# Attention with 16-feature heads: three banks for the scores by key and one for the output, in place of two and two

## The reference

```
# block 1 (stage Aatt): 4 batch entries, T = 1024, 16 heads of 16 features, rotary positions, causal
att = jnp.einsum('bhqd,bhkd->bhqk', q, k) / jnp.sqrt(jnp.float32(HS))
att = jnp.where(causal, att, jnp.float32(-1000000000.0))
att = jax.nn.softmax(att, axis=-1)
y = jnp.einsum('bhqk,bhkd->bhqd', att, v)
...
# block 3 (stage Catt): the same sizes, no mask, a bias by relative position
att = jnp.einsum('bhqd,bhkd->bhqk', q, k) * (1.0 / math.sqrt(HS))
att = att + compute_bias(rel_emb, t, t)
att = jax.nn.softmax(att, axis=-1)
o = jnp.einsum('bhqk,bhkd->bhqd', att, v)
```

## Time and profile before

| | us |
|---|---|
| median of 3 timed runs (lowest to highest) | 7709.58 (7699.38 to 7716.36) |
| profiled execution, its own time | 7715.76 |
| its span, first to last instruction | 7714.1 |
| Aatt, scores from the first to the last start | 287.8 to 956.6 |
| Catt, scores from the first to the last start | 3105.7 to 4032.4 |
| busy in the whole span: PE, DVE, ACT, POOL | 6384.6, 4755.7, 2770.5, 1252.2 |

### The profile page before, as it was taken

One profiled execution on the slowest core, in us unless ns is written; L12 is line 12 of the kernel. 1 busy time (PEld: TensorE's weight loads), 2 busy tenths in 40 slices (PEclk: granted clock), 3 DMA queues, 4 the chain that ended last, 5 costly groups with the idle time before them and its releaser, 6 DMA issues. The chain is left out here.

```text
span 7714.1 us, 120187 instructions
## 1 busy us (share of the span) xinstructions
PE 6384.6 (83%) x31364; PEld 3277.2 (42%) x31364; DVE 4755.7 (62%) x12029; ACT 2770.5 (36%) x6066; POOL 1252.2 (16%) x779
## 2 busy tenths in 40 slices
PE   6788858989987976899994387887996888998979
PEld 2333334655455533222222263334553455544555
DVE  4656557733763534899985747984335764347635
ACT  0255514712463210466661104541110354224611
POOL 1100016100620002000000003550002431015100
PEclk9899979989998988899997599998998999999999
DMA  5422245541455245333323211114222455324541
GB/s 176 115 64 65 54 132 155 181 141 59 147 169 185 75 176 199 103 81 76 87 55 108 90 70 53 37 39 132 66 63 83 132 163 175 93 88 147 170 149 55
DMA packets 931101, 850.48 MB, mean 110 GB/s; under 512 B 222216, under 2 KB 785377, under 8 KB 930465
## 3 DMA queue, kind: packets, MB, share of 16 engines
q1 hardware_dynamic: 500624, 522.99, 23.7%
q10 hardware_dynamic: 430080, 323.08, 13.1%
HBM read 503.10 MB, written 346.00 MB: 110 GB/s over the span
## 5 line engine op out<-in xcount | busy, mean ns | idle before, releaser
L1252 ACT ACTIVATE Catt_E<-Catt_t 128x512 f32<-128x512 f32 x1024 | 576.3, 595 | 341.2 <-DVE Catt_t L1215 259.9
L1189 DVE CUSTOM_DVE_ANT_0 Catt_S<-Catt_s,Catt_win 128x1024 f32<-128x1024 f32 x512 | 621.5, 1215 | 6.9 <-DMA Catt_win<-skewed 5.4
L1189 DVE CUSTOM_DVE_ANT_0 Aatt_S<-Aatt_s,Aatt_win 128x128 f32<-128x128 f32 (+7 forms) x512 | 375.4, 756 | 250.6 <-PE Aatt_s L1118 245.0
L1252 ACT ACTIVATE Aatt_E<-Aatt_t 128x512 f32<-128x512 f32 (+3 forms) x768 | 353.8, 489 | 283.5 <-PE Aatt_t L1150 177.4
L1147 PE MATMUL Catt_t<-Catt_Q,Catt_K 123*128 123x512 bf16 x1024 | 369.7, 388 | 58.2 <-ACT Catt_E L1252 28.3
L1118 PE MATMUL Catt_s<-Catt_K,Catt_Q 96*128 96x512 bf16 x1024 | 320.9, 396 | 25.4 <-DMA Catt_K<-k_parts 12.5
L1215 DVE TENSOR_TENSOR Catt_t<-Catt_t,Catt_near 128x256 f32<-128x256 f32 (+2 forms) x640 | 281.7, 457 | 75.1 <-PE Catt_t L1147 67.6
L1169 PE MATMUL Catt_o<-Catt_E,Catt_V 128*32 128x256 f32 x4096 | 327.9, 392 | 0.0
L1147 PE MATMUL Aatt_t<-Aatt_Q,Aatt_K 99*128 99x512 bf16 (+3 forms) x768 | 245.2, 337 | 63.4 <-ACT Aatt_E L1252 34.6
L2343 PE MATMUL scan_cum<-scan_X,scan_upto 128*128 128x512 f32 x512 | 265.6, 609 | 24.7 <-DVE scan_X L2412 23.3
L2341 PE MATMUL scan_cum<-scan_X,scan_after 128*128 128x512 f32 x448 | 240.6, 619 | 44.1 <-DVE scan_pi L2423 44.1
(11 more groups left out here) (721 smaller groups left out, 14466.6 us busy)
## 6 DMA issues: line engine op xcount, KB each, us to landing
moe_cb<-c_s SPq DMA_DIRECT2D x16, 1024.0 KB
bias_rows<-line SPq DMA_DIRECT2D x16, 960.0 KB, 6.5
skewed<-bias_win ACTq DMA_DIRECT2D x16, 960.0 KB
Catt_win<-skewed SPq DMA_DIRECT2D x16, 960.0 KB, 4.8
rec<-state_in_r ACTq DMA_DIRECT2D x32, 416.0 KB
scan_r<-rec SPq DMA_DIRECT2D x64, 208.0 KB, 2.5
Aatt_Q<-q_parts SPq DMA_DIRECT2D x32, 384.0 KB, 4.3
Aatt_K<-k_parts SPq DMA_DIRECT2D x32, 384.0 KB, 5.4
```

The costliest lines, as they stand in the source:

```text
L1189: v.tensor_tensor_reduce(out=S[:, j % 2, 0:w], in0=s_ps[j % 2][:, 0:w], in1=win[:, 0 if causal else h, w0:w0 + w], scale=-1.0, scalar=BIG, ...
L1252: a.activation(E[:, kb % NB, h, lo:hi], t_ps[n % 2][:, 0:hi - lo], ACT.Exp, scale=scale).then_inc(exped, 1)
```

## The change

Each of the eight banks is kept in use, but `t_ps` becomes three banks and `o_ps` one. Units rotate through three banks and a unit waits for the exponential of unit n - 3. The number of units of a pair is 96 in Aatt, a multiple of three, and 128 in Catt, whose numbering therefore goes on over the pairs. The turned maxima take the bank of the unit that follows them, as before. The first value product of an entry waits until the output of the entry just before was copied out.

```diff
-        t_ps = [pl.ps(f"t{i}") for i in range(2)]
-        o_ps = pl.ps("o", (P, T))
+        t_ps = [pl.ps(f"t{i}") for i in range(3)]
+        o_ps = pl.ps("o")
...
+        def bank(it, n):
+
+            return t_ps[(n if causal else it * nt + n) % 3]
... turn_maxima
-                t.wait_ge(exped, it * nt + (n - 1 + PRIMED))
-                t.matmul(t_ps[n % 2][0:2 * PARTS * NT, 0:P], parts[:, b % 2].rearrange("p h k u -> p (h k u)"), ident_b[:],
+                t.wait_ge(exped, it * nt + (n - 2 + PRIMED))
+                t.matmul(bank(it, n)[0:2 * PARTS * NT, 0:P], parts[:, b % 2].rearrange("p h k u -> p (h k u)"), ident_b[:],
... scores_by_key
-                    t.wait_ge(exped, it * nt + (n - 1 + PRIMED))
+                    t.wait_ge(exped, it * nt + (n - 2 + PRIMED))
                     diagonal = causal and lo == kb * P
-                    ins = t.matmul(t_ps[n % 2][:, 0:hi - lo], K[:, b, h, kb * P:(kb + 1) * P], Q[:, b, h, lo:hi],
+                    ins = t.matmul(bank(it, n)[:, 0:hi - lo], K[:, b, h, kb * P:(kb + 1) * P], Q[:, b, h, lo:hi],
... values
-                        f, o = quadrant(h, x), b % 2 * CH
-                        ins = t.matmul(o_ps[f:f + 2 * hd, o + k0 * P:o + k1 * P], V[:, b, kb, h, :], blocks[:, h, x, k0:k1, :],
+                        f = quadrant(h, x)
+                        ins = t.matmul(o_ps[f:f + 2 * hd, k0 * P:k1 * P], V[:, b, kb, h, :], blocks[:, h, x, k0:k1, :],
... scalar engine
-            a.sem_inc(o_moved, 2)
+            a.sem_inc(o_moved, 1)
... move_out
-                a.activation(O[:, b, :], o_ps[:, b % 2 * CH:(b % 2 + 1) * CH], ACT.Copy).then_inc(o_moved, 1)
+                a.activation(O[:, b, :], o_ps[:], ACT.Copy).then_inc(o_moved, 1)
                 a.wait_ge(r_out, it * (16 * B) + (16 * b + 16))
-                a.wait_ge(o_moved, it * B + (b + 3))
+                a.wait_ge(o_moved, it * B + (b + 2))
```

More of the change, by code:

```diff
@@ L1144, in scores_by_key @@
                 for c, lo, hi, n, _ in units[i]:
-                    t.wait_ge(exped, it * nt + (n - 1 + PRIMED))
+                    t.wait_ge(exped, it * nt + (n - 2 + PRIMED))
                     diagonal = causal and lo == kb * P
-                    ins = t.matmul(t_ps[n % 2][:, 0:hi - lo], K[:, b, h, kb * P:(kb + 1) * P], Q[:, b, h, lo:hi],
+                    ins = t.matmul(bank(it, n)[:, 0:hi - lo], K[:, b, h, kb * P:(kb + 1) * P], Q[:, b, h, lo:hi],
                                    start=True, stop=not diagonal)
                     if diagonal:
-                        ins = t.matmul(t_ps[n % 2][:, 0:P], ident_b[:], near[:], start=False, stop=True)
+                        ins = t.matmul(bank(it, n)[:, 0:P], ident_b[:], near[:], start=False, stop=True)
                     ins.then_inc(t_done, 1)
@@ L1213, in add_near @@
                     v.wait_ge(t_done, it * nt + (n + 1))
-                    x = t_ps[n % 2][:, a - lo:z - lo]
+                    x = bank(it, n)[:, a - lo:z - lo]
                     v.tensor_tensor(x, x, near[:, b, h, a - (kb - 1) * P:z - (kb - 1) * P], ALU.add).then_inc(near_done, 1)
@@ L1241, in move_maxima @@
                 a.wait_ge(m_out, it * (16 * B) + (16 * b + 16))
-                a.activation(turned[:, b % 2, :], t_ps[behind_sums(b) % 2][0:2 * PARTS * NT, 0:P], ACT.Copy).then_inc(m_moved, 1)
+                a.activation(turned[:, b % 2, :], bank(it, behind_sums(b))[0:2 * PARTS * NT, 0:P], ACT.Copy).then_inc(m_moved, 1)
             def exp(it, i):
@@ L1251, in exp @@
                     a.wait_ge(pv_done, it * nv + (last_values(i, c) + 1 + nv))
-                    a.activation(E[:, kb % NB, h, lo:hi], t_ps[n % 2][:, 0:hi - lo], ACT.Exp, scale=scale).then_inc(exped, 1)
+                    a.activation(E[:, kb % NB, h, lo:hi], bank(it, n)[:, 0:hi - lo], ACT.Exp, scale=scale).then_inc(exped, 1)
             def move_out(it, i):
```

## The result

The changed kernel takes 7730.36 us (median of 8 runs, 7727.82 to 7739.49) against 7709.38 (8 runs, 7696.65 to 7716.36); the ratio is 1.0033, 95% interval 1.0023 to 1.0043, so it is 18 to 33 us slower. The prediction had 7782 us, a loss of 72. The sign was right and the size was not: the time lies next to its rival (1), 7736 us, but not for the reason that this rival gave. The ratio gives a difference of 25 us and the two medians one of 21.

What follows compares the result with a forecast made beforehand. VectorE was taken to bound Catt, a chain through TensorE's queue Aatt. Catt 41 - 8 - 7 = +26, Aatt 14 - 14 = 0, clock +46: +72 on 7709.58, 7782 us; range 7750 to 7810, 8 in 10 7700 to 7832.

Steps and rivals of the forecast that it cites:

- rival (1): Both stages: the stall costs what was worked out but the clock holds; +26 us, 7736 us, chance 0.22.
- The output bank: Entry changes: value product waits for ScalarE's output copy; net +1.35 us each in Catt (+41), +0.44 in Aatt (+14).
- The clock: Falls behind the new pauses: 21 in Catt, 10 in Aatt, 1.47 us each, +46 us.
- the walk: Step-by-step timing from profile rows: Catt's entry change +1.35 us net, Aatt's +0.44, Catt's tail step 1.28 us.
- rival (2): Both stages: third bank gives more, the pause costs less, Catt's net wait under 1.2 us; -21 us, 7689, chance 0.10.
- Catt's tail: Catt's last 44 us, without masks: three banks cut the step from 1.68 to 1.28 us, -7 us.
- The third bank: Scores by key: removes waits of 0.25 us in Catt (-8 us) and 0.58 in Aatt (-14), besides the tail.

Runs made afterwards that it cites:

- one_out: Kernel before with one output bank but still two banks for the scores by key; 7815.54 us against 7706.69, ratio 1.0138.
- The fill: Changed kernel plus six products never read, queued on TensorE ahead of its wait for the output copy; 7681.63 us against 7706.69 before, ratio 0.9965.
- The mask experiment: Kernel before with Catt's mask and maximum over 768 of 1024 columns; 7697.4 us against 7712.68, ratio 0.9978.

## Why the prediction was right or wrong

**The output bank: right.** The pairing of the value product with the copy of its own step and the net cost came out, at 1.34 us per entry in Catt and 0.43 in Aatt when that half ran alone, for 1.35 and 0.44. That they agree to 0.01 is in part luck: the walk in Catt supposed three banks for the scores by key, and one_out has two.

**The clock: right in kind, too few falls in Catt.** 27 in the steady stretch (29 in all from the first copy of maxima to the last) and not 21 there, 8 more in Aatt and not 10, 1.46 us each for 1.47: about +51 us for the +46. The fill shows that a fall is a cost of its own and not a name for the stall. Of rival (1) the number came out but the reason, a clock that holds, did not. Of rival (2) one half was so, a third bank that gives more than the walk says, and the other, a net wait per entry under 1.2 us, was not.

**Catt's tail: right in the sum, in part by luck.** -7.3 us for -7, though its step became 1.10 us and not the 1.28 of the walk:

```profile
4089.34 0.57 DVE L1219 TENSOR_TENSOR Catt_t<-Catt_t,Catt_near 128x384 f32<-128x384 f32 x1 [0.54 <-PE Catt_t L1151]
4090.44 0.57 DVE L1219 TENSOR_TENSOR Catt_t<-Catt_t,Catt_near 128x384 f32<-128x384 f32 x1 [0.54 <-PE Catt_t L1151]
```

The tail's own change of entry, with a wait of 1.70 us and a fall of the clock behind it, took back a part of that larger gain.

**The third bank: this is the step that failed.** I took "-8 us" from it in Catt and "-14" in Aatt; the halves apart show 31 x 1.19 = -37 and 31 x 1.29 = -40. The missing 55 us are the whole error: +72 less 55 is +17, beside a measured 21 to 25. The cause was one sentence: "So VectorE bounds Catt, and 1.3 us per period is all that freer banks could give there". I read an engine without a listed wait as one that is full. It was held back by 0.07 us in about half of the steps, and by more in a few, by the ring through two banks, and the ring's length, 1.68 us, stood in the earlier trace rows and equals the spacing of the value products in steady Catt, 3499.80 to 3501.48, on which the walk was built. The mask experiment shows it: with a quarter of the mask's columns gone, VectorE keeps the same step. In the entry of one_out without a fall, eight of 16 gaps from a mask to what follows it are 1.20 or 1.21 us, one is 1.34 and one 1.47, where the changed kernel has 1.14 each time; together with 0.06 at the turned maxima that is 1.1 of the 1.19. Of all this I had credited the 1.47 alone, at 0.25. The ring also had a row of its own in the view of waits that the earlier trace rows was taken from. It stands with TensorE's weight loads and not with VectorE, for the same 200 us before (first row) and after:

```profile
PEld Catt_t L1147 <- ACT Catt_E L1252: 66.7, 159, 1.6
```

```profile
PEld Catt_t L1151 <- ACT Catt_E L1256: 20.4, 47, 1.2
```

The loads for the scores by key waited for exponentials 159 times before, beside the 22 waits of VectorE on which I built, and 47 times after. In Aatt I credited the one wait that I had a row for, 0.58 us, and rightly: the product in its place, at 588.70 in the changed kernel, has no wait in front of it. The other half lies in eight exponentials that follow each other without a listed wait:

```profile
591.10 4.46 ACT L1252 ACTIVATE Aatt_E<-Aatt_t 128x512 f32<-128x512 f32 x8 [0.65 <-PE Aatt_t L1150]
```

```profile
578.79 3.82 ACT L1256 ACTIVATE Aatt_E<-Aatt_t 128x512 f32<-128x512 f32 x8 [0.65 <-PE Aatt_t L1154]
```

4.46 us before (first row) and 3.82 after, for the same eight. 0.64 and 0.58 make 1.22 of the 1.29; the split is read from one entry each.

The Trainium skill, Perfetto Trace Analysis, Matmuls, says that groups of products should rotate through banks so that the copying out of one lies beside the next. Both halves bear it out, and I weighed them wrongly: by the runs, the third bank gives 77 us of steady time, and giving up the second output bank costs 31 x (1.34 + 0.43) = 55 before the clock.

**The sum.** Aatt -17 (predicted +14 - 14 + 15 = +15), Catt +44 - 7 (predicted +57 in all). Adding up what the halves gave: 55 - 77 - 7 + 51 = +22, and 21 to 25 was measured. The 55 and the 77 are both read from the intervals of three kernels (before, one_out and the changed one), so this sum checks the intervals and not the split between the two halves.

## What to carry to other kernels

Two instructions back to back on an engine do not prove that the engine is full: divide the stretch by the steps and compare it with the length of each ring through a buffer (product, addition, exponential, product in the same bank). Where the two agree to 0.01 us, as 1.68 and 1.68 here, take it that the ring sets the pace, whatever engine looks busy, and test it by giving that engine less to do. Look also at who waits for the release of the buffer, the weight loads included. When a buffer is taken away, look at where its release stands in the releasing engine's own queue: moving that one copy ahead of two exponentials turned a loss of 0.3% into a gain of 1.5%. A stall of TensorE has to be priced with the fall of its clock behind it, and products that nobody reads can be cheaper than the pause.

## What the runs showed of the hardware that was not expected

- Instructions of VectorE and of ScalarE overlap in the records when nothing holds them: mask to addition is 1.14 us where one mask takes 1.22, and eight exponentials take 3.82 us (0.48 each) where one of 512 columns takes 0.60. So a gap of 0.07 us can be a wait that no row of that engine names.
- A pause of TensorE of 2.2 us between stretches at full work was followed by a fall of its granted clock to the 1.2 GHz level at nearly every entry of Catt, in 29 of 31 intervals, at 1.46 us each. Filled so that 0.63 us of it were left it brought none there; with 0.59 left after the copy was moved, 1. In one_out the pause, 1.78 us, brought falls in 23 of 31. What tells the ones with a fall from those without was not tried.
